# Routing of two mixture-of-experts layers: marks and held values in 16-bit parts, weights listed later, norms moved ahead

## The reference

```
# layer 0: 8 experts, width 512, one shared expert
logits = xf @ router_w.T + experts_bias
rw, sel = top_k(logits, 2);  rw = softmax(rw)
out = sum over the two experts e of rw[e] * (silu(xf@w1[e]) * (xf@w3[e])) @ w2[e]  + shared(xf)
# layer 1: 8 experts, width 1024
m, sel = top_k(logits, 2)
mult1 = softmax(logits, masked where (m1-logits)/max(|logits|,m1) > 0.02)[sel1]
mult2 = the same about m2, without expert sel1
out = mult1 * expert(sel1) + mult2 * expert(sel2)
```

## Time and profile before

| | us |
|---|---|
| median of 3 runs | 1884.54 (1882.66 to 1884.92) |
| the profiled execution's own time | 1883.69 |
| its span, first to last instruction | 1881.9 |
| layer 0's mixture, first statistics | 386.79 |
| layer 0, transposes of the first gathered block | 524.95 |
| layer 1's mixture, first statistics | 1366.79 |
| layer 1, first gate matmul | 1452.59 |
| TensorE / VectorE / ScalarE / GpSimd busy | 85% / 65% / 49% / 33% |

### The profile page before, as it was taken

One profiled execution on the slowest core, in us unless ns is written; L12 is line 12 of the kernel. 1 busy time (PEld: TensorE's weight loads), 2 busy tenths in 40 slices (PEclk: granted clock), 3 DMA queues, 4 the chain that ended last, 5 costly groups with the idle time before them and its releaser, 6 DMA issues. The chain is left out here.

```text
span 1881.9 us, 32646 instructions
## 1 busy us (share of the span) xinstructions
PE 1593.4 (85%) x11328; PEld 1155.5 (61%) x11328; DVE 1218.0 (65%) x2035; ACT 930.5 (49%) x1746; POOL 625.7 (33%) x863
## 2 busy tenths in 40 slices
PE   4889986858899997588888977887747999999996
PEld 2445443558899997233333332222247999999995
DVE  3566552444578886477777468777764777777773
ACT  1345452122156664145545657667711666666662
POOL 5444420010036654633344334333011233333321
PEclk8899998968899999689999988887855999999998
DMA  5222211121158885522212312222033677677763
GB/s 139 49 44 57 47 36 34 56 67 37 49 170 234 231 236 132 132 65 41 52 40 57 64 33 62 48 48 51 1 114 117 192 210 219 198 208 217 199 185 84
DMA packets 192834, 200.21 MB, mean 106 GB/s; under 512 B 33121, under 2 KB 167778, under 8 KB 192642
## 3 DMA queue, kind: packets, MB, share of 16 engines
q1 hardware_dynamic: 156578, 155.12, 28.0%
q0 software_dynamic: 36096, 43.04, 12.2%
HBM read 139.52 MB, written 22.54 MB: 86 GB/s over the span
## 5 line engine op out<-in xcount | busy, mean ns | idle before, releaser
L648 ACT ACTIVATE l1a_sb_probs<-l1a_s_ps,l1a_sb_kmax 128x512 f32<-128x512 f32 x256 | 173.0, 701 | 83.5 <-issue 52.2
L1668 PE MATMUL l1m_g_ps<-l1m_sb_rows_hi,l1m_sb_hi 128*128 128x256 f32 x736 | 209.2, 284 | 1.4 <-DVE l1m_sb_rows_lo L1550 1.4
L1668 PE MATMUL l1m_g_ps<-l1m_sb_rows_hi,l1m_sb_lo 128*128 128x256 f32 x736 | 208.9, 284 | 0.0
L1668 PE MATMUL l1m_g_ps<-l1m_sb_rows_lo,l1m_sb_hi 128*128 128x256 f32 x736 | 208.9, 284 | 0.0
L452 POOL DMA_DIRECT2D l1a_sb_kst<-l1a_sb_hi x256 | 125.7, 496 | 248.2 <-PE l1a_s_ps L768 197.6
L549 DVE TENSOR_REDUCE l1a_sb_mx<-l1a_s_ps 128x2 f32<-128x1024 f32 x128 | 154.0, 1219 | 62.2 <-PE l1a_s_ps L731 62.0
L583 DVE TENSOR_REDUCE l1a_sb_kmax<-l1a_s_ps 128x2 f32<-128x1024 f32 x128 | 153.0, 1217 | 41.1 <-PE l1a_s_ps L768 40.8
L654 ACT ACTIVATE l1a_sb_probs<-l1a_s_ps 128x1024 f32<-128x1024 f32 x128 | 128.0, 1023 | 88.3 <-PE l1a_s_ps L768 87.9
L768 PEld LDWEIGHTS l1a_s_ps<-l1a_sb_qst,l1a_sb_kst 49*128 49x128 f32 (+1 forms) x512 | 50.4, 197 | 176.2 <-issue 94.2
L549 DVE TENSOR_REDUCE l0a_sb_mx<-l0a_s_ps 128x2 f32<-128x256 f32 (+3 forms) x128 | 103.4, 821 | 80.1 <-PE l0a_s_ps L742 78.7
L768 PE MATMUL l1a_s_ps<-l1a_sb_qst,l1a_sb_kst 49*128 49x512 f32 (+1 forms) x512 | 131.0, 518 | 28.4 <-ACT l1a_sb_probs L648 23.7
(11 more groups left out here) (339 smaller groups left out, 4198.6 us busy)
## 6 DMA issues: line engine op xcount, KB each, us to landing
l1m_sb_raw<-in_l1m_w SPq DMA_DIRECT2D x184, 256.0 KB, 3.6
l0m_sb_raw<-in_l0m_w SPq DMA_DIRECT2D x96, 256.0 KB, 3.6
l1m_sb_raw<-in_l1m_w SPq DMA_DIRECT2D x23, 1024.0 KB, 6.4
l0m_sb_raw<-in_l0m_w SPq DMA_DIRECT2D x24, 512.0 KB, 4.7
l1a_sb_qst<-l1a_sb_hi SPq DMA_DIRECT2D x256, 32.0 KB, 2.1
l1a_sb_kst<-l1a_sb_hi POOLq DMA_DIRECT2D x256, 32.0 KB, 2.0
l0a_sb_qst<-l0a_sb_hi SPq DMA_DIRECT2D x128, 32.0 KB, 2.1
l0a_sb_kst<-l0a_sb_hi POOLq DMA_DIRECT2D x128, 32.0 KB, 2.1
```

The source lines that it names most:

```text
L648: ins = act.activation(probs[:, n % 8, e, :], at[:, e, :], ACT.Exp, bias=kmax[:, n % 4, e:e + 1], accum_out=zsum[:, n % 4, e:e + 1])
L1668: ins = pe.matmul(at, s, m, start=n == 0, stop=n == len(passes) - 1)
```

## The change

Three things, in both layers unless said.

1. The marks (`spots`), `own`, `upto`, `row_at` and `held` become bfloat16. Held values are five in place of two: the token's number as tile x 128 and as place in the tile, and the weight as three bfloat16 parts that add up to it (`share`). The marks of all four quarters have room of their own, so VectorE no longer waits for TensorE between them.
2. In layer 1 the list is made in two parts. The tokens (46 columns) come at once; the exponents and weights come after the gather is issued, and their list (69 columns, into `y_ps`) is made by TensorE behind the first gate chunk. As the first half of the marks lies in `raw2`, the first w2 is loaded only after that list (`first_w2` on SyncE), and is split (CV) after chunk 1.
3. In layer 0 all norms come ahead of the shared blocks' gates, and the first block's rows are split before the second batch is transposed. LOGITS 0 and the last two TURNs come after chunk 0, LOGITS 1 to 3 after chunk 1.

```diff
 def moe_schedule(shared, nf):          # layer 0 (shared)
-        yield "C", 0, 0
-        yield from normed(1)           # LN1 2, LN2 1, TURN 1
-        yield "LOGITS", 0, 0
+    LN1 0, LN1 1, LN2 0, TURN 0, LN1 2, LN2 1      # both layers
+        C 0 0, T 0, TURN 1, LN1 3, LN2 2, C 0 1, CV, LN2 3
-        between = {0: [*normed(2), ("LOGITS", 1, 0)],
-                   1: [*normed(3, True), ("LOGITS", 2, 0)],
-                   2: [("LOGITS", 3, 0), ("R", TOP1, 0)], ...
-                   5: [("EXP", 0, 0), ("R", EXPERTS, 0), ("LOAD", 0, 0)],
-                   6: [("R", WEIGHTS, 0)],
-                   7: [("R", PLACES, 0)],
-                   8: [("R", SPOT, 0)]}
+        between = {0: [("TURN", 2, 0), ("LOGITS", 0, 0), ("TURN", 3, 0)],
+                   1: [("LOGITS", b, 0) for b in range(1, B)],
+                   2: [("TOP1", 0, 0)], ...
+                   5: [("EXP", 0, 0), ("EXPERTS", 0, 0), ("LOAD", 0, 0)],
+                   6: [("SHARES", 0, 0), ("ROWS", 0, 0)],
+                   7: [("PLACES", 0, 0), ("HELD", 0, 0)],
+                   8: [("WEIGHTS", 0, 0), ("SPOT", 0, 0)]}
         for c in range(1, NSPOT):
-            between[8 + c] = [("SPOT", c - 1, 0), ("R", SPOT + c, 0)]
+            between[8 + c] = [("LIST", c - 1, 0), ("SPOT", c, 0)]
...
+        # layer 1, after LOGITS 3
+        for step in ("TOP1", "TOP2", "RANK", "EXPERTS", "LOAD", "ROWS", "PLACES", "HELD"):
+            yield step, 0, 0
+        for c in range(NSPOT):
+            yield "SPOT", c, 0
+            yield "LIST", c, 1
+        UNMASKED 0, EXP 0, LISTS, GATHER, C 0 0, UNMASKED 1, EXP 1, C 0 1, T 0, SHARES, WEIGHTS, C 0 2, C 0 3
+        between = {0: [("LIST", c, 2) for c in range(NSPOT)], 1: [("WEIGHED", 0, 0), ("CV", 0, 0)]}

+            spots = [t.bitcast(BF16)...   # layer 1: raw2 and late[:, 2:4]
+        held = sb("held", [P, TOP, NTILE, 5, NBLK], BF16)

+            def first_w2(*_):             # SyncE, at WEIGHED
+                if not shared:
+                    sp.wait_ge(weights_listed, 1)
+                    load_w2(0, expert(0))

+    def shares(*_):                       # after the weights themselves
+        whole = full("weight")
+        for n in range(3):
+            part = at["share"][:, :, :, n]
+            then(dve.tensor_copy(part, whole))
+            if n < 2:
+                then(dve.tensor_tensor(full("less"), whole, part, ALU.subtract))
+                whole = full("less")
+    def held_tokens(*_):
+        for k in range(TOP):
+            then(dve.scalar_tensor_tensor(held[:, :, 0, :], iota tiles, float(P), own, ALU.mult, ALU.mult))
+            then(dve.tensor_scalar(held[:, :, 1, :], own, const["token"][:, 0:1], None, ALU.mult))
+    def held_weights(*_):
+        for k in range(TOP):
+            for n in range(3):
+                then(dve.tensor_tensor(held[:, k, :, 2 + n, :], own, share n over NBLK, ALU.mult))
+    def spot(c, _):
+        dve.tensor_tensor(spots[k][:, tiles, :], span_b over SPOTS, row_at over BLK, ALU.is_equal)
+    def row_weights(*_):                  # WEIGHED
+        copy the three parts out of PSUM, two adds
```

More of the change, by code:

```diff
@@ L1079 @@
 NBLK = (B * T * TOP - E) // BLK + E
-TOP1, TOP2, BELOW, EXPERTS, WEIGHTS, PLACES = range(6)
-SPOT, LISTS = 6, 6 + NSPOT
 class Tally:
@@ L1094, in wait @@
             eng.wait_ge(self.sem, value)
[L1097 to L1102, removed]
+ALL, TOKENS, WEIGHTS = slice(0, 5), slice(0, 2), slice(2, 5)
+PARTS = (ALL, TOKENS, WEIGHTS)
 def moe_schedule(shared, nf):
@@ L1128, in moe_schedule @@
         for c in range(1, NSPOT):
-            between[8 + c] = [("SPOT", c - 1, 0), ("R", SPOT + c, 0)]
-        between[8 + NSPOT] = [("SPOT", NSPOT - 1, 0), ("R", LISTS, 0), ("GATHER", 0, 0)]
-    else:
[L1132 to L1136, removed]
+            between[8 + c] = [("LIST", c - 1, 0), ("SPOT", c, 0)]
+        between[8 + NSPOT] = [("LIST", NSPOT - 1, 0), ("LISTS", 0, 0), ("GATHER", 0, 0), ("WEIGHED", 0, 0)]
+    else:
+        yield "TURN", 1, 0
+        yield "LOGITS", 0, 0
+        yield "LN1", 3, 0
+        yield "LN2", 2, 0
+        yield "TURN", 2, 0
+        yield "LOGITS", 1, 0
+        yield "LN2", 3, 0
+        yield "TURN", 3, 0
+        yield "LOGITS", 2, 0
+        yield "LOGITS", 3, 0
+        for step in ("TOP1", "TOP2", "RANK", "EXPERTS", "LOAD", "ROWS", "PLACES", "HELD"):
[3 more added lines that the diff above has]
+            yield "LIST", c, 1
+        yield "UNMASKED", 0, 0
@@ L1137, in moe_schedule @@
         yield "EXP", 0, 0
-        yield "R", TOP2, 0
-        yield "RANK", 0, 0
-        yield "R", BELOW, 0
+        yield "LISTS", 0, 0
+        yield "GATHER", 0, 0
+        yield "C", 0, 0
+        yield "UNMASKED", 1, 0
         yield "EXP", 1, 0
[L1142 to L1148, removed]
-        yield "C", 0, 0
@@ L1700, in output, with route @@
                     ins.then_inc(y_ready.sem, 1)
-            run({"TURN": turn, "LOGITS": logits, "RANK": rank, "SPOT": lists, "T": turn_rows, "G": hidden,
+            run({"TURN": turn, "LOGITS": logits, "RANK": rank, "LIST": lists, "T": turn_rows, "G": hidden,
                  "Y": output})
-def route(dve, then, const, phi, at, sems):
+def route(dve, then, const, phi, weights_ps, at, sems):
     def full(t):
@@ new lines, in row_weights @@
+    def row_weights(*_):
+        if phi:
+            dve.wait_ge(sems["weights_listed"], 1)
+        then(dve.tensor_copy(at["row_holds"][:, :, WEIGHTS, :], weights_ps[:, :, WEIGHTS, :]))
+        dve.sem_inc(sems["weighed"], 1)
+        then(dve.tensor_tensor(full("row_weight"), at["row_holds"][:, :, 2, :], at["row_holds"][:, :, 3, :], ALU.add))
+        then(dve.tensor_tensor(full("row_weight"), full("row_weight"), at["row_holds"][:, :, 4, :], ALU.add))
+    return {"TOP1": top1, "TOP2": top2, "UNMASKED": unmasked, "EXPERTS": experts, "SHARES": shares, "ROWS": rows,
+            "PLACES": places, "HELD": held_tokens, "WEIGHTS": held_weights, "SPOT": spot, "LISTS": lists,
+            "WEIGHED": row_weights}
```

296 lines of the change are left out of this document (167 added, 129 removed).

## The result

The changed kernel takes 1842.99 us (median of 4 runs, 1838.35 to 1845.17) where the kernel before takes 1884.73 beside it: a ratio of 0.9773 [0.9759, 0.9788]. It is faster by 41.7 us; I had said 28.7, in the range 1841 to 1869. The profiled execution took 1841.51 us.

What follows compares the result with a forecast made beforehand. TensorE was taken as the bound, behind serial chains with VectorE at half clock in each layer's front. Layer 0's 23.5 us and layer 1's 5.2 sum to 28.7 off, giving 1856 us, range 1841 to 1869.

Steps and rivals of the forecast that it cites:

- The forecast's own range: Whole kernel: the span 1850 to 1861 us given to the forecast itself, with chance 0.48.
- an early clock in the front: Layer 0's front: the clock rises early, gain 22 us for 15.4; part of the range's low end.
- marks at half the time: Both layers: 16-bit marks and weight products at half the time, 8.7 us more gain; chance 0.15.
- Layer 0's front: Layer 0 up to the end of the third chunk's gates: stalls go, gain 15.4 us (13 to 22).
- My own bound of 22: Layer 0's front: upper end of the 13 to 22 us bounds on its gain of 15.4 us.
- X to T8: Layer 0, third chunk's gates' end to the first gathered block's transposes: 82.5 us becomes 74.4, gain 8.1 (3 to 12).
- Marks at 2.28: Both layers: 16-bit marks keep the float32 row's 2.28 us, as one input is read again and again.
- rival 1: Both layers: 16-bit marks and weight products run at half the time, 8.7 us more gain, 1847; chance 0.15.
- Layer 1 to H0: Layer 1 up to its first gates: shorter work before the gather brings them 22.8 us earlier.
- H0 to block 1's gates: Layer 1, first gates to block 1's gates: 29.3 us, with TensorE idle 9.5 awaiting w2, then 2.0 for half clock.
- rival 3: Layer 0's front gains less, from half clock throughout or copies holding TURN 3: 15 us in layer 0, 1864; chance 0.12.

Runs made afterwards that it cites:

- The front alone: The kernel before, with only layer 0's new front order of norms, transposes and logits put in: 1863.68 us, ratio 0.9884 to the kernel before.

## Why the prediction was right, and where its sizes were off

The mechanism was right: two serial fronts, a shorter one in each layer, and most of layer 1's given back in a wait for w2. The sum was 28.7 and is 42.2 by the spans: layer 0 35.7 (23.5 said), layer 1 7.5 (5.2 said), the rest -1.0 in stretches that vary by themselves. The forecast's own range, 1850 to 1861, missed by 7 us. That 1842.99 lies inside the stated range, 1841 to 1869, owes something to luck: that end had been reckoned from an early clock in the front (6.6 us, which came) and from marks at half the time (8.7 us, which did not). What came in their place, cheaper lists and stretches of clock, had no part in it.

- **Layer 0's front: 15.4 said, 23.1 measured (55.6 to 32.5). This term was mis-sized, and it is over half of the error.** The order was read rightly: first gates 10.5 us from the stage's start (397.3 - 386.79 = 10.5 said), no stall but 0.99 ahead of TURN 3. The error is in "the clock was lost again around the logits, so I take 427": I took the fall of the old front, which has gaps of 4 to 6 us before every TURN, for one that the logits bring at once. With the gaps gone, the clock came in the first chunk and was lost for 3.5 us only, behind the long row of logits. The front alone shows the same, so it owes nothing to the 16-bit parts. My own bound of 22 was 1.1 short.
- **X to T8: 8.1 said, 12.6 measured.** SPOT 0 ended 42.8 us after X (42.1 said), and the stall was 7.60 (8 said). That sum left out two of the four token products (+1.1 us), and gave the 16-bit parts 0.4 where they took off 0.8. From the first list to T8 it took 27.1 us, not 32.3. From start to start, as I had counted, the lists are 1.5 + 3 x 0.83 = 4.0 us, not 7.9: a quarter is 8 places x 2 halves, 16 matmuls, and the earlier trace rows shows x32 because a float32 matmul is there twice. I kept the 32, as the kernel's description did. The price of one was near, 0.83 / 16 = 52 ns for the 48 said. The other 1.3 us fit the clock: gates and outputs between the lists took 25.2 us before and 23.1 now, 2.1 less where I had taken off 0.8. The same two stretches before and after (first list to T8):

```profile
482.77:524.95 42.18, 42.18 (x309) 0.84 0.09 26
```

```profile
463.79:490.89 27.10, 27.10 (x245) 0.92 0.11 32
```

At half clock stood 2 x 0.16 x 42.2 = 13.5 us before and 4.3 after.
- **Marks at 2.28: right**, and for the reason given; rival 1 is out. `own` fell from 0.92 to 0.57 us and one of each two token products from 0.54 to 0.33, inside the bound.
- **Layer 1 to H0: 22.8 said, 24.0 measured**; the gather 54.5 from the stage's start (55 said).
- **H0 to block 1's gates: 29.3 said, 28.8 measured.** LIST 2 took 2.05 us, not 4.2, by the same factor of two; w2 was issued at H0 + 18.2 (18.3 said), waited for till H0 + 24.8, TensorE idle 11.0 us (9.5 said), and half clock behind it (0.75 over the next 5.7 us), which cost 1.4 us up to the first output (2.0 said). The two kernels with an earlier load confirm that most of this wait was the order of SyncE's queue.
- No rival came; one execution of eleven went some way towards rival 3. That w2's load could be moved and give 8.7 us back was in none of them.

## What to carry to other kernels

Before a matmul count is taken from a trace, divide by what the source's loops issue: a wide type can stand there twice, and changing the type changes both the price and the count. A load that frees a stage late costs what its place in the issuing engine's queue costs; look there before blaming bandwidth. And with two stretches of low clock in a front, give the new order a price at the clock of work without gaps as well as at the clock the gaps had left.

## What the runs showed of the hardware

- A row of 48 matmuls of 8 columns, 5.4 us, that stands behind gates without a gap, was followed by 3.4 us at 1.2 GHz in nine traces of nine, and one of 32 (3.64 us) in one of one. Behind 16 of them (1.85 us) the clock stayed in these ten traces; in an eleventh it fell soon after them and again within the row of 48.
- A comparison on 16-bit operands takes 1.23 us for 2048 elements, 2.29 with one input of step 0, and 8 x 0.21 for 256 each with the value as an operand per partition.
- Beside GpSimd's products, 0.87 us for 368 elements, VectorE's took about twice their time (1.18 and 0.75 us for 0.54 and 0.33).
- The rows of the first two gathers had arrived 4.7 us after the first was issued with no DMA traffic in the 8 us ahead, and 8.2 us after it with 3 MB of weights issued around them.
